# Other neighbours on the matrix engine in the first attention of a two-layer transformer kernel

## The reference

```python
h = _layernorm(x) * (1 + ca) + sa
x = rmsnorm(h, norm_w)
q = (x @ Wq)            # 16 heads of 64
k, v = x @ Wkv          # 8 heads of 64 each
q, k = l2norm(q) * ..., l2norm(k) * ...     # per head
sim = tanh(q k^T / 50) * 50 * 64 ** -0.5, causal
out = softmax(sim) @ v, the two query heads of a key head summed
x = x + ga * (out @ Wout)
```

## Time and profile before

| | us |
|---|---|
| median of 3 runs (lowest, highest) | 1972.01 (1971.07, 1972.77) |
| the profiled execution, its span | 1968.78, 1966.9 |
| first attention stage, first to last score group's tanh | 50.2 to 896.2 |

### The profile page before, as it was taken

One profiled execution on the slowest core, in us unless ns is written; L12 is line 12 of the kernel. 1 busy time (PEld: TensorE's weight loads), 2 busy tenths in 40 slices (PEclk: granted clock), 3 DMA queues, 4 the chain that ended last, 5 costly groups with the idle time before them and its releaser, 6 DMA issues. The chain is left out here.

```text
span 1966.9 us, 41395 instructions
## 1 busy us (share of the span) xinstructions
PE 1906.3 (97%) x14878; PEld 1320.6 (67%) x14878; DVE 1589.5 (81%) x3897; ACT 1444.5 (73%) x2052; POOL 688.2 (35%) x956
## 2 busy tenths in 40 slices
PE   7999999999999999998999999999999988999998
PEld 5788888888888888886444444777777753444443
DVE  7888888888888888865767775788888877888886
ACT  4888888888888888885677776566666655666665
POOL 1555555555555555552000000355555540000000
PEclk8999999999999999999999999999999998999999
DMA  3501111101111011100765553100000000000000
GB/s 100 128 15 28 28 28 28 26 17 28 28 28 28 18 25 28 25 23 17 174 138 123 120 110 75 44 2 1 2 2 2 2 2 6 12 11 17 12 17 17
DMA packets 57001, 75.67 MB, mean 38 GB/s; under 512 B 9456, under 2 KB 34144, under 8 KB 56672
## 3 DMA queue, kind: packets, MB, share of 16 engines
q1 hardware_dynamic: 56800, 73.03, 15.6%
HBM read 51.47 MB, written 4.77 MB: 29 GB/s over the span
## 5 line engine op out<-in xcount | busy, mean ns | idle before, releaser
L513 PE MATMUL a_pS<-qs,k 128*128 128x256 f16 x1536 | 376.2, 273 | 4.2 <-issue 3.0
L533 PEld LDWEIGHTS a_pO<-va,pr 128*128 128x128 f32 x2048 | 321.4, 191 | 82.1 <-issue 72.9
L533 PE MATMUL a_pO<-va,pr 128*128 128x66 f32 x2048 | 331.2, 251 | 3.1 <-DVE on L857 2.5
L1974 ACT ACTIVATE c_pr<-c_pS 128x1536 f32<-128x1536 f32 x128 | 185.8, 1451 | 105.6 <-PE c_pS L1772 105.6
L1083 POOL TENSOR_SCALAR_AFFINE_SELECT pr<-pr 128x512 f32<-128x512 f32 x256 | 181.2, 731 | 192.6 <-ACT pr L1009 192.6
L1001 ACT ACTIVATE th<-a_pS 128x1536 f32<-128x1536 f32 x128 | 185.6, 1450 | 66.6 <-PE a_pS L513 63.7
L2018 POOL TENSOR_SCALAR_AFFINE_SELECT c_pr<-c_pr 128x512 f32<-128x512 f32 x256 | 175.7, 714 | 129.0 <-DVE c_pr L1862 129.0
L513 PEld LDWEIGHTS a_pS<-qs,k 128*128 128x128 f16 x1536 | 195.6, 131 | 7.8 <-issue 4.6
L864 POOL TENSOR_TENSOR qp<-qg,qp 128x1024 f16<-128x1024 f32 x64 | 149.2, 2332 | 120.5 <-ACT qp L977 120.5
L1009 ACT ACTIVATE pr<-th 128x1536 f32<-128x1536 f32 x128 | 189.5, 1481 | 1.1
L535 PEld LDWEIGHTS a_pO<-va,pr 128*128 128x128 f32 x1024 | 161.8, 191 | 31.4 <-issue 28.7
(11 more groups left out here) (264 smaller groups left out, 4334.5 us busy)
## 6 DMA issues: line engine op xcount, KB each, us to landing
b_cwB<-b_by_expert SPq DMA_DIRECT2D x64, 512.0 KB, 8.4
k<-k SPq DMA_DIRECT2D x64, 256.0 KB, 3.7
x<-in_L_attn_tokens_dram SPq DMA_DIRECT2D x8, 512.0 KB, 7.0
out_dram<-x SPq DMA_DIRECT2D x16, 256.0 KB, 2.3
mb<-a_by_sample SPq DMA_DIRECT2D x31, 128.0 KB, 3.5
d_h<-in_L_ffn_h_w_dram SPq DMA_DIRECT2D x2, 1024.0 KB, 8.2
c_gb<-c_by_sample SPq DMA_DIRECT2D x1, 2048.0 KB, 7.0
b_by_expert<-b_cwT SPq DMA_DIRECT2D x64, 8.0 KB, 1.4
```

What stands on the lines that cost most here:

```text
L513: last = pe.matmul(out, (k1, k2)[part][k][:, h // G2, keys * P:(keys + 1) * P], q, start=part == 0, stop=part == 1)
L533: last = pe.matmul(out, w[:, hh * N + t * P:hh * N + (t + 1) * P], v[:, 0, p, :], start=True, stop=t == 0)
L1974: act.activation(pr[g][:, :, :], pS[:, :, 0:N + P], ACT.Exp, scale=float(1.0 / np.sqrt(np.float32(DQ)))).then_inc(s_ex, 1)
```

## The change

The same operations on the same data. Three things differ:

- The order inside each engine's loop body (PE, DVE, ACT, POOL), and where the body begins: it now starts in the middle of the former one (PE at score 2 of group 2).
- Which of the three `pW` banks a step writes.
- With the banks, what PE waits for before it overwrites one.

Banks and a part of the waits (`...` marks what is left out):

```diff
-        QK_BANK = (1, 0, 1, 1, 0, 2)
+        QK_BANK = (1, 0, 1, 2, 1, 2)
         QT_BANK = (1, 0, 0, 2)
-        KT_BANK, V_BANK, HB_BANK = (1, 0), (1, 1), (2, 2)
-        X_BANK, O_BANK, BACK_BANK = 1, 2, 2
+        KT_BANK, V_BANK, HB_BANK = (0, 2), (0, 1), (2, 1)
+        X_BANK, O_BANK, BACK_BANK = 0, 2, 0
...
         def pe_project_qk(pe, n, m):
...
+            elif m == 1:
+                if n >= 1:
+                    pe.wait_ge(s_va, 2 * n - 1)
...
+            elif m == 2:
+                if n >= 3:
+                    pe.wait_ge(s_at, 2 * n - 4)
...
             elif m == 3:
                 if n >= 1:
+                    pe.wait_ge(s_ks, 2 * n)
...
             else:
+                pe.wait_ge(s_qg, 6 * n + 4)
```

The loop body of PE after the change, whole for the samples in the middle (the body before stands above):

```diff
             for n in range(-3, B + 2):
+                pe_score(pe, n, 2, 2)
+                pe_weigh(pe, n, 0, 3)
+                pe_score(pe, n, 2, 3)
+                pe_weigh(pe, n, 0, 4)
+                pe_score(pe, n, 2, 4)
                 pe_project_qk(pe, n + 2, 1)
+                pe_weigh(pe, n, 0, 5)
+                pe_score(pe, n, 2, 5)
                 pe_heads_back(pe, n - 1, 0, 1)
+                pe_weigh(pe, n, 0, 6)
+                pe_score(pe, n, 2, 6)
                 pe_heads_back(pe, n - 1, 0, 2)
                 pe_heads_back(pe, n - 1, 0, 3)
                 pe_weigh(pe, n, 0, 7)
+                pe_score(pe, n, 2, 7)
...
                 pe_heads_back(pe, n - 1, 1, 0)
                 pe_heads_back(pe, n - 1, 1, 1)
                 pe_heads_back(pe, n - 1, 1, 2)
                 pe_heads_back(pe, n - 1, 1, 3)
                 pe_weigh(pe, n, 0, 8)
+                for m in range(8, 11):
+                    pe_score(pe, n, 2, m)
+                    pe_weigh(pe, n, 0, m + 1)
                 pe_score(pe, n, 2, 11)
                 pe_project_qk(pe, n + 2, 2)
...
                 pe_out_project(pe, n - 1, 0)
+                pe_out_project(pe, n - 1, 1)
+                pe_out_project(pe, n - 1, 2)
+                pe_out_project(pe, n - 1, 3)
                 pe_weigh(pe, n, 1, 0)
+                pe_score(pe, n, 3, 0)
                 pe_weigh(pe, n, 1, 1)
...
                 pe_turn_k(pe, n + 1, 0)
+                for m in range(1, 6):
+                    pe_score(pe, n, 3, m)
+                    pe_weigh(pe, n, 1, m + 1)
...
                 pe_turn_k(pe, n + 1, 1)
+                pe_score(pe, n, 3, 6)
                 pe_weigh(pe, n, 1, 7)
...
                 pe_turn_q(pe, n + 1, 0)
+                pe_score(pe, n, 3, 7)
+                pe_out_back(pe, n - 1, 0)
+                pe_weigh(pe, n, 1, 8)
                 pe_score(pe, n, 3, 8)
+                pe_out_back(pe, n - 1, 1)
+                pe_weigh(pe, n, 1, 9)
                 pe_score(pe, n, 3, 9)
+                pe_project_qk(pe, n + 2, 3)
+                pe_weigh(pe, n, 1, 10)
                 pe_score(pe, n, 3, 10)
+                pe_weigh(pe, n, 1, 11)
...
                 pe_turn_q(pe, n + 1, 1)
                 pe_score(pe, n, 3, 11)
                 pe_project_qk(pe, n + 2, 4)
                 pe_project_qk(pe, n + 2, 5)
...
                 pe_weigh(pe, n, 2, 0)
+                pe_score(pe, n + 1, 0, 0)
+                pe_weigh(pe, n, 2, 1)
+                pe_score(pe, n + 1, 0, 1)
+                pe_weigh(pe, n, 2, 2)
+                pe_score(pe, n + 1, 0, 2)
                 pe_transpose_x(pe, n + 3, 0)
                 pe_transpose_x(pe, n + 3, 1)
...
+                pe_weigh(pe, n, 2, 3)
+                for m in range(3, 11):
                     pe_score(pe, n + 1, 0, m)
+                    pe_weigh(pe, n, 2, m + 1)
+                pe_score(pe, n + 1, 0, 11)
                 pe_project_qk(pe, n + 3, 0)
...
                 pe_weigh(pe, n, 3, 0)
+                pe_turn_q(pe, n + 1, 2)
+                pe_turn_q(pe, n + 1, 3)
+                for m in range(0, 11):
+                    pe_score(pe, n + 1, 1, m)
+                    pe_weigh(pe, n, 3, m + 1)
+                pe_score(pe, n + 1, 1, 11)
+                pe_values(pe, n + 2, 0)
+                pe_heads_back(pe, n, 0, 0)
+                pe_values(pe, n + 2, 1)
+                pe_weigh(pe, n + 1, 0, 0)
+                pe_score(pe, n + 1, 2, 0)
+                pe_weigh(pe, n + 1, 0, 1)
+                pe_score(pe, n + 1, 2, 1)
+                pe_weigh(pe, n + 1, 0, 2)
```

More of the change, by code:

```diff
@@ L404, in pe_values @@
             if t == 0:
+                if n >= 1:
+                    pe.wait_ge(s_qs, 4 * n - 1)
+                else:
+                    pe.wait_ge(s_hT, n + 2)
+            else:
                 if n + 1 < B:
@@ L455, in pe_turn_k @@
                 if n + 1 < B:
[L456 to L460, removed]
                     pe.wait_ge(s_qg, 6 * n + 8)
                 else:
-                    pe.wait_ge(s_qs, 4 * n - 1)
+                    pe.wait_ge(s_va, 2 * n + 1)
+            else:
+                if n >= 2:
+                    pe.wait_ge(s_og, n - 1)
+                elif n >= 1:
+                    pe.wait_ge(s_qs, 4 * n)
+                else:
+                    pe.wait_ge(s_qg, 6 * n + 6)
             out = pW[KT_BANK[t]][:, :].bitcast(F16)
@@ L474, in pe_turn_q @@
             if i == 0:
-                pe.wait_ge(s_ks, 2 * n + 1)
+                if n + 1 < B:
+                    pe.wait_ge(s_qg, 6 * n + 9)
+                else:
+                    pe.wait_ge(s_at, 2 * n - 2)
             elif i == 1:
-                pe.wait_ge(s_ks, 2 * n + 2)
+                if n >= 2:
+                    pe.wait_ge(s_st, 3 * n - 5)
+                else:
+                    pe.wait_ge(s_ks, 2 * n + 1)
             elif i == 2:
-                if n + 1 < B:
-                    pe.wait_ge(s_qg, 6 * n + 11)
+                if n + 2 < B:
+                    pe.wait_ge(s_hT, n + 3)
                 else:
@@ L547, in pe_heads_back @@
                     else:
-                        pe.wait_ge(s_st, 3 * n - 2)
+                        pe.wait_ge(s_og, n)
                 else:
-                    pe.wait_ge(s_at, 2 * n + 1)
+                    if n + 2 < B:
+                        pe.wait_ge(s_va, 2 * n + 6)
+                    elif n + 1 < B:
+                        pe.wait_ge(s_qs, 4 * n + 5)
+                    else:
+                        pe.wait_ge(s_at, 2 * n)
             last = pe.transpose(pW[HB_BANK[t]][:, j * P:(j + 1) * P], as_[:, t, j * P:(j + 1) * P], c.id32[:, :])
@@ L579, in pe_out_back @@
                 pe.wait_ge(s_og, n + 1)
-                pe.wait_ge(s_og, n + 1)
+                if n + 2 < B:
+                    pe.wait_ge(s_ks, 2 * n + 5)
+                elif n + 1 < B:
+                    pe.wait_ge(s_qs, 4 * n + 7)
+                else:
+                    pe.wait_ge(s_st, 3 * n - 2)
             last = pe.transpose(pW[BACK_BANK][:, t * P:(t + 1) * P], og[:, t * P:(t + 1) * P], c.id32[:, :])
@@ L935, in _ @@
                 dve_add(dve, n - 1)
+                dve_outputs(dve, n, 2)
+                dve_ln(dve, n + 3, 1)
+                dve_gain(dve, n + 2, 3)
+                dve_measure(dve, n - 1, 1)
                 dve_take_q(dve, n + 1, 1)
-                dve_measure(dve, n - 1, 1)
+                dve_outputs(dve, n, 3)
+                dve_gain(dve, n + 2, 4)
+                dve_mean_square(dve, n + 2)
             dve.wait_ge(s_st, ADD_STEPS * B)
```

183 lines of the change are left out of this document (45 added, 138 removed).

## The result

| | before | after |
|---|---|---|
| median of four runs each (lowest, highest), us | 1971.54 (1970.05, 1972.77) | 1960.09 (1957.11, 1962.21) |
| profiled execution, its span, us | 1968.78, 1966.9 | 1957.11, 1955.2 |
| first attention stage, first to last tanh, us | 50.17 to 896.24 | 50.72 to 885.00 |
| median period of a sample, us | 26.894 | 26.358 |

The ratio is 0.9941, with a 95% interval of 0.9924 to 0.9958: 11.5 us or 0.59% faster. The prediction said 1955.5 and 16.5 us.

A forecast was written before the change was run, and what follows sets the result against it. PE's own sequence and waits were taken as the bound; 0.78 - 0.28 + 0.05 = 0.55 us per sample, times 30 samples, gave 16.5 us and a forecast of 1955.5 us, range 1945.5 to 1968.

The forecast's parts named there:

- 15 bare loads at 0.052: On PE, 15 fp32 weight loads per sample, uncovered behind calls or query turns, become hidden: 0.78 us per sample gained.
- Rival (c): On PE, loads don't hide under a score or these neighbours, so the 0.78 falls away: 1972 us; chance 0.06.
- The wait for the keys: At a sample's first score, PE waits 0.28 us for the swapped key DMAs, before 0.05; gives back 0.23.
- rival (a): At a sample's first score, the key copies come in time, so the whole gain stays: 1947.1 us; chance 0.13.
- The other queues at nothing: ScalarE, VectorE, GpSimd and SP do the same work in another order and keep up: cost taken as nothing.
- (b): At handoffs with little to spare, one more wait of 0.1 to 0.3 per sample: 1959 to 1965 us; chance 0.17.
- (d): At the narrow gaps between score groups, tanh becomes the bound: 20 us slower, 1992 us; chance 0.10.
- 0.25 to spare at the fourth projection: On PE, the fourth projection, now waiting for the second key half's copy, has 0.25 us of slack: no cost.
- The 0.19 at the tanh: Between score groups, the shortest new distance 2.00 exceeds the needed 1.81, leaving 0.19 us if ScalarE is free: no cost.
- The net, 0.55 per sample: Per sample in the first attention stage: 0.78 - 0.28 + 0.05 = 0.55 us gained.
- Those rare ones stay and cancel: At a sample's first score, rare longer key DMA waits, about 1.1 us, are the same before and after: no net cost.
- Start and end of the stage: At both ends of the first attention stage, the same chain in turned loops: 0, with 1.5 us either way.

The follow-up runs named there:

- 1: Kernel after, with PE's wait for the swapped key copy moved from a sample's first score to its second: 1949.03 us, ratio 0.9893.
- 7: Kernel before, with PE's wait for the swapped key copy moved from a sample's first score to its second: 1967.6 us, ratio 0.9984.
- 4: Kernel after, with score, call, score, call regrouped as score, score, call, call at nine places per sample: 1971.19 us, ratio 1.0005.
- 3: Kernel after, with the second key turn two scores and two calls earlier: 1945.26 us, ratio 0.9875.
- 5: Kernel after, with a sample's first-group scores reordered, three reading the plain key copy first, and the swapped-copy wait at the fourth: 1943.04 us, ratio 0.9851.
- 2: Kernel after, with the second key turn one score and one call later: 1964.39 us, ratio 0.997.
- 6: Kernel after, with plain-key scores first, swapped-copy wait at the fourth, and second key turn two scores and two calls earlier: 1943.63 us, ratio 0.9856.

## Why the prediction was right, and where it was too high

**What bounds the kernel**: right. PE is still the bound at 99.43 of 100 us, and each experiment moved the time through PE's steps or waits.

**15 bare loads at 0.052**: right, 0.78 forecast and 0.775 measured by 1 and 7 (PE's steps are 26.842 before and 26.067 after; 26.86 and 26.08 had been taken); 4 shows the single load. A sample holds 48 calls of two passes each, four groups of twelve, and not 96; the sum counts neighbours and does not use that number. The choice of 0.86 for a projection behind a score, between 0.86 and 0.91, was right. Rival (c), that loads don't hide, falls with that. The rule of the Trainium skill's "TensorE: Matmul & The Clock Gate", Part 3, The mechanism, that a load overlaps only with another row group, does not agree with these runs: all loads here use all rows, and nine calls cost 0.472 more per sample when their loads stand behind a call instead of a score. The same section also names a background weight buffer as a case in which a load is pulled ahead; what the runs show is in line with that case.

**The wait for the keys**: right in place, cause and size. 0.28 forecast, 0.291 measured; the path 6.10 forecast, 6.08 in the row above; 0.09 and not 0.06 from landing to score (this sample's second DMA took 3.75 and landed at 655.33). So rival (a), keys in time, fell, though 1, 3 and 5 show that it was one wait or a few reordered scores away.

**The other queues at nothing**: right for the samples in the middle, where no score waits for a tanh and no projection for a copy; rivals (b) and (d) did not come about there. The 0.25 to spare at the fourth projection were 0.17: 2 used 0.28 and was late by 0.11. The 0.19 at the tanh were not tried in the middle.

**The net, 0.55 per sample**: 0.536 measured.

**From the sample to the run: here it failed.** From 16.5 forecast to 11.67:

- "So 30 samples" counted two too many. The samples with the full gain are the 28 middle periods; the two others give nothing: 1.1. The rate of 0.536 takes another 0.4.
- "Those rare ones stay and cancel" was wrong by 2.06. In the middle samples the landings of the second key DMA that stood out were 3.93, 4.42, 4.51 and 4.60 before, and 3.89, 4.36, 4.39, 4.64, 4.77 and 5.12 after. Above the usual 3.78 they hold 2.3 and 4.5, nearly the two excesses (2.57 and 4.63): with a path without slack, before and after, each is paid in full, and after there were more and longer ones. One longer wait has another source: in the sample whose second key DMA is issued at 309.69 before and 304.51 after, SP issued the first one 0.46 after the copy's end instead of 0.07. All nine traces have this delay in that sample; why is not shown. The sizes are shown for these two executions alone. The runs after spread over 5.1 us, those of 5 over 2.4, so this term probably varies from run to run; it was one to be bounded, not cancelled.
- "Start and end of the stage ... I take 0, with 1.5 either way": measured 1.40 lost by the four terms listed above, 1.27 with the smaller pieces, inside the bound. The largest piece is the last period, and 1.62 of it is the granted clock, which fell to 0.50 in the last sample; the prediction had no term for that, having read the clock in the middle alone. The two waits for the tanh, which the order on PE could have told, are not what makes it long: they are the same 1.83 in 5 and 6 (0.48 and 1.35), and there the last periods are 22.95 and 22.76, below the 23.34 of before.

The scale was right: after's median lies 2.98 above its profiled execution, 3.2 had been taken. The time lies where rival (b) was priced, though the mechanism of (b) is not what took it there.

## What to carry to other kernels

Where the matrix engine is full, read the distance of starts of neighbouring steps, not their durations: a step's price can depend on what stands in front of it, and a change of order alone is then worth the sum over neighbours. Before regrouping, list each transfer whose slack is about zero, and add up both the path and the work that is left beside it; here that gave the new wait to 0.01 us, and the remedy, to let the work that doesn't need the transfer go first, brought another 17 us beside the 11.5 of the regrouping. Count the samples in which the gain really occurs, and look at the last one separately: a filler taken from the next sample is missing there, and the granted clock has to be read there too; here it fell to half, which cost 1.6 us that no count of neighbours contains.

## What the runs showed of the hardware

**Long landings and instruction fetches.** The key DMAs' packets in the sample of the row at 549.44, from first issue to landing, and in an ordinary sample (queue, kind: packets, MB, share of 16 engines):

```profile
DMA packets 305, 0.67 MB, mean 122 GB/s; under 512 B 48, under 2 KB 176, under 8 KB 304
q1 hardware_dynamic: 304, 0.66, 48.3%
q8 instruction: 1, 0.02, 1.3%
```

```profile
DMA packets 304, 0.66 MB, mean 143 GB/s; under 512 B 48, under 2 KB 176, under 8 KB 304
q1 hardware_dynamic: 304, 0.66, 57.8%
```

The one thing more in the window of the long landing is a packet with instructions, 16 KB. Over the nine kernels' traces (28 samples each, without the first two and the last two) the second key DMA took 3.66 to 3.82 in all 187 samples without such a packet in its window. With one, it took 3.55 to 5.16 in 65 samples, 28 of them above 4.2. So every long landing coincides with a fetch, though not every fetch makes one. That the fetch delays the keys is argued from this coincidence; no run moved a fetch on purpose, and why some do no harm stays open.

**GpSimd beside VectorE.** In the kernel after, GpSimd's sum of two heads (L1088) stands beside VectorE's long product. Both in order of time:

```profile
664.99 1.75 DVE L840 TENSOR_TENSOR qg<-qg,rr 128x1536 f32<-128x1536 f32 x1
...
665.16 1.90 POOL L1088 TENSOR_TENSOR as<-on 128x128 f32<-128x128 f32 x1 [1.44 <-DVE on L851]
667.37 0.49 POOL L1088 TENSOR_TENSOR as<-on 128x128 f32<-128x128 f32 x1 [0.32 <-DVE on L851]
```

The same sum takes 1.90 beside the product and 0.49 after it; it ends at 667.06, 0.32 after the product's end. The Trainium skill's "SBUF — State Buffer", Who interferes with whom, says that a VectorE instruction with two SBUF inputs contends with a GpSimd instruction that reads SBUF. These rows agree with it (both factors of the product and the sum's heads lie in SBUF), but no run took the product away. On the page the mean of this line rose from 455 to 636 ns, while the causal zeros (L1083 before, L1077 after) fell from 731 to 637, having other neighbours too; the prediction had taken these engines' work as unchanged by a new order. Here it cost nothing, since the transposes that need the sums stand several steps later on PE, and no wait for GpSimd shows on PE in the middle samples.
